# Head sums on four column tiles, constants issued behind x, and the pair's mean taken off by VectorE

## What is computed

```python
x = x + local_attention(_gn(x), ...)       # pool, q k v, 3 x 3 neighbours, softmax, gate, projection
x = x + deformable_conv(_gn(x), ...)       # offsets and masks by a 3 x 3 conv, sampling, ReLU

def _gn(v, G=32, eps=1e-05):               # 64 channels in 32 groups: pairs of channels
    m = jnp.mean(g, axis=(2, 3, 4), keepdims=True)
    s = jnp.var(g, axis=(2, 3, 4), keepdims=True)
    return ((g - m) / jnp.sqrt(s + eps)).reshape(v.shape)

attn = jnp.einsum('bhwnd,bhwknd->bhwnk', qh, kp) * scale    # 8 heads of 8 channels, k: 9 taps
attn = jax.nn.softmax(attn, axis=-1)
out = jnp.einsum('bhwnk,bhwknd->bhwnd', attn, vp)
```

## Time and profile before

| | us |
|---|---|
| median of 3 runs | 197.28 (196.97 to 197.58) |
| profiled execution | 197.45 |
| its span, first to last instruction | 195.4 |
| busy in the span: PE | 174.9 |
| DVE | 152.3 |
| ACT | 103.8 |
| POOL | 86.1 |
| granted TensorE clock, mean over the span | 0.992 |

### The profile page before, as it was taken

How to read it: one execution, slowest core, us unless ns; L and a number is a source line. 1 busy time by engine, 2 the same in 40 slices (tenths; PEclk the granted TensorE clock), 3 DMA queues, 4 the chain that set the end, 5 groups by cost and what they waited for, 6 DMA issues and landing times.

```text
span 195.4 us, 4621 instructions
## 1 busy us (share of the span) xinstructions
PE 174.9 (90%) x1822; PEld 123.9 (63%) x1822; DVE 152.3 (78%) x256; ACT 103.8 (53%) x195; POOL 86.1 (44%) x103
## 2 busy tenths in 40 slices
PE   0299996997979998999999999999989999999990
PEld 0224963653436544547687999658668788998870
DVE  0899958996559798984989988517998897979920
ACT  1136228610002796559877888447938868786000
POOL 8334983569020339504534618403733617536000
PEclk9999999999999999999999999999999999999996
DMA  5950000000040011305551000000012100000000
GB/s 182 351 42 4 3 0 0 3 0 0 0 107 3 27 28 41 98 26 125 122 124 41 15 3 0 3 0 3 9 30 55 37 7 11 0 17 2 20 0 24
DMA packets 10325, 7.66 MB, mean 39 GB/s; under 512 B 5175, under 2 KB 8773, under 8 KB 10297
## 3 DMA queue, kind: packets, MB, share of 16 engines
q1 hardware_dynamic: 9913, 6.35, 12.8%
q10 hardware_dynamic: 288, 0.89, 1.4%
q0 software_dynamic: 96, 0.06, 0.1%
HBM read 2.82 MB, written 0.52 MB: 17 GB/s over the span
## 4 chain that ended last, share of the span: by engine, by line
PE 66%; DVE 14%; ACT 8%; issue 4%; DMA 3%; POOL 2%; SPq 0%; DVEq 0%; POOLq 0%
PE ps L1267 20%; PE ps L1241 11%; PE ps L1161 10%; PE ps L1310 6%; PE ps L1057 4%; DVE smp_prod L801 3%; DMA x_parts<-in_x 3%; PE ps L1226 3%; PE ps L1094 3%; PE ps L1212 2%; ACT disty L616 2%; PE ps L1178 2%; ACT haty L621 1%; PE ps L1025 1%; ACT hx_selx L629 1%
## 5 line engine op out<-in xcount | busy, mean ns | idle before, releaser
L912 DVE TENSOR_TENSOR smp_prod<-ps,hx_selx 128x768 f32<-128x768 f32 x72 | 67.4, 951 | 10.0 <-PE ps L1241 9.2
L1267 PE MATMUL ps<-smp_prod,windows_attention 128*64 128x192 f32 (+2 forms) x512 | 54.9, 337 | 0.1
L1267 PEld LDWEIGHTS ps<-smp_prod,windows_attention 128*64 128x64 f32 x512 | 38.3, 136 | 5.8 <-DVE windows_attention L897 0.4
L1241 PE MATMUL ps<-haty,by_rows 128*64 128x256 f16 x432 | 39.1, 274 | 1.3 <-DVE smp_prod L912 1.2
L476 POOL TENSOR_SCALAR disty<-disty 64x512 f32<-64x512 f32 (+1 forms) x23 | 12.8, 556 | 57.5 <-ACT haty L621 57.4
L1241 PEld LDWEIGHTS ps<-haty,by_rows 128*64 128x64 f16 x432 | 26.6, 109 | 6.4 <-issue 2.7
L629 ACT ACTIVATE hx_selx<-ps 128x512 f32<-128x512 f32 x36 | 21.3, 591 | 16.2 <-PE ps L1226 16.2
L483 POOL TENSOR_TENSOR haty<-disty,haty 64x512 f16<-64x512 f32 (+1 forms) x23 | 24.0, 1043 | 1.9
L1161 PE MATMUL ps<-conv_staged 128*108 128x512 f32 (+1 forms) x60 | 23.3, 521 | 0.7 <-ACT x_parts L593 0.6
L631 ACT ACTIVATE hx_selx<-hx_selx 128x512 f32<-128x512 f32 x36 | 22.7, 631 | 1.1
L926 DVE TENSOR_TENSOR vals_attw<-ps,windows_attention 128x384 f32<-128x384 f32 x24 | 13.3, 555 | 7.1 <-PE ps L1267 4.4
(11 more groups left out here) (139 smaller groups left out, 253.1 us busy)
## 6 DMA issues: line engine op xcount, KB each, us to landing
windows_attention<-windows_attention SPq DMA_DIRECT2D x8, 256.0 KB, 3.8
x_parts<-in_x SPq DMA_DIRECT2D x2, 256.0 KB, 5.2
bcast<-in_bcast SPq DMA_DIRECT2D x2, 256.0 KB, 6.7
x2seq<-x_parts SPq DMA_DIRECT2D x4, 128.0 KB, 2.6
out<-x_parts SPq DMA_DIRECT2D x16, 32.0 KB, 2.0
vals_attw<-in_cf ACTq DMA_DIRECT2D x1, 480.0 KB, 5.8
stack_m<-x_parts SPq DMA_DIRECT2D x12, 36.0 KB
kept<-in_cf ACTq DMA_DIRECT2D x1, 390.5 KB, 4.3
```

The costliest lines, as they stand in the source:

```text
L912: nc.vector.tensor_tensor(pairs, rows, cols.unsqueeze(1).to_broadcast([P, QUARTERS, HW]), ALU.mult).then_inc(s_mult, 1)
L1241: ins = nc.tensor.matmul(ps[h * C:(h + 1) * C, at:at + HW], by_matrix(a, QUARTERS - 1 - k)[:, h * C:(h + 1) * C], haty[i % 2][:, p * HW:(p ...
L1267: return nc.tensor.matmul(dst[:, at:at + strips * 3 * SP].rearrange("p (s k n) -> p s k n", k=3, n=SP), rows, sampled(i, ki, m, first, str ...
```

## The change

1. SP issues `kept` and `attw` right behind x; ScalarE's queue no longer does.
2. In `logits` the four matmuls of a group go to four column tiles (image of the pair and half of the pixels give the tile). The two pairs c now add into the same rows, so that the first matmul in a bank sets `start` and those of c = 1 add to it. `spread` picks its matrices and halves accordingly.
3. The matmul with `gnd` goes. VectorE subtracts its own mean from the pair's mean in PSUM, and copies the pair's mean and variance without waiting for that copy until its last step.

```diff
@@ sync
             for c in range(2):
                 sp.dma_start(xin[:, c * BANK:(c + 1) * BANK], x[:, c * BANK:(c + 1) * BANK]).then_inc(s_x[c], 16)
+            sp.dma_start(kept[:, :], cf[:, 0:kept.shape[1]]).then_inc(s_kept, 16)
+            sp.dma_start(attw, cf[:, kept.shape[1]:]).then_inc(s_cst, 16)
             sp.dma_start(bcast[:, 2 * DG * P:], sel16["bcast"][:, 3 * DG * P:]).then_inc(s_bcast, 16)
@@ scalar
-            act.dma_start(kept[:, :], cf[:, 0:kept.shape[1]]).then_inc(s_kept, 16)
-            act.dma_start(attw, cf[:, kept.shape[1]:]).then_inc(s_cst, 16)
@@ vector, norm
                 dve.wait_ge(s_pair, n)
-                link(nc.vector.tensor_copy(pair[:, :], bank(7)[:, 0:4 * J]))
-                gap = pair[:, 2 * J:4 * J].rearrange("p (j s) -> p j s", s=2)[:, :, 0]
+                own_mean = meanvar[:, :].rearrange("p (j s) -> p j s", s=2)[:, :, 0]
+                mean = bank(7)[:, 0:2 * J].rearrange("p (j s) -> p j s", s=2)[:, :, 0]
+                gap = pair[:, 2 * J:3 * J]
                 var = pair[:, 0:2 * J].rearrange("p (j s) -> p j s", s=2)[:, :, 1]
+                link(nc.vector.tensor_tensor(gap, mean, own_mean, ALU.subtract))
+                nc.vector.tensor_copy(pair[:, 0:2 * J], bank(7)[:, 0:2 * J]).then_inc(s_paircopied, 1)
                 link(nc.vector.tensor_tensor(gap2[:, :], gap, gap, ALU.mult))
+                dve.wait_ge(s_paircopied, n)
@@ tensor, pair_stats
-                nc.tensor.matmul(bank(7)[:, 0:2 * J], gnp, meanvar[:, :], start=True, stop=True)
-                nc.tensor.matmul(bank(7)[:, 2 * J:4 * J], gnd, meanvar[:, :], start=True, stop=True).then_inc(s_pair, 1)
+                nc.tensor.matmul(bank(7)[:, 0:2 * J], gnp, meanvar[:, :], start=True, stop=True).then_inc(s_pair, 1)
@@ tensor, logits
+            FIRST_OF_BANK = (0, TAPS - POOL_TAPS, TAPS - 1)
...
-                for part in range(2):
-                    for j in (2 * c, 2 * c + 1):
-                        ins = nc.tensor.matmul(ps[32 * j:32 * j + 32, t * HF:(t + 1) * HF],
-                                               cst["headsum"][:, 32 * part:32 * part + 32],
-                                               prod[:, t * N + j * HW + part * HF:][:, 0:HF], start=(part == 0),
-                                               stop=(part == 1), skip_group_check=True)
+                for j in (2 * c, 2 * c + 1):
+                    for part in range(2):
+                        rows = 32 * (2 * (j % 2) + part)
+                        ins = nc.tensor.matmul(ps[rows:rows + 32, t * HF:(t + 1) * HF],
+                                               cst["headsum"][:, 32 * c:32 * c + 32],
+                                               prod[:, t * N + j * HW + part * HF:][:, 0:HF], start=(c == 0 and t in FIRST_OF_BANK),
+                                               stop=(c == 1), skip_group_check=True)
@@ tensor, spread
                 for i in range(2 * J):
-                    at = (2 * DG + i % J) * P
+                    j, part = divmod(i, 2)
+                    at = (2 * DG + 2 * part + j // 2) * P
                     ins = nc.tensor.matmul(ps[:, PB[pos % 3] * BANK + i * HF:][:, 0:HF], bcast[:, at:at + P],
-                                           halves[i // J][:, t * HF:(t + 1) * HF], start=True, stop=True)
+                                           halves[j % 2][:, t * HF:(t + 1) * HF], start=True, stop=True)
```

More of the change, by code:

```diff
@@ L150, in bass_local_attention_then_deformable_conv @@
         meanvar = sb("meanvar", [P, 2 * J])
-        pair = sb("pair", [P, 4 * J])
+        pair = sb("pair", [P, 3 * J])
         gap2 = sb("gap2", [P, J])
@@ L282, in bass_local_attention_then_deformable_conv @@
         s_bn = sem("s_bn")
-        s_kept, s_bcast, s_byd, s_selxd, s_own = sem("s_kept"), sem("s_bcast"), sem("s_byd"), sem("s_selxd"), sem("s_own")
+        s_kept, s_paircopied, s_bcast, s_byd, s_selxd, s_own = sem("s_kept"), sem("s_paircopied"), sem("s_bcast"), sem("s_byd"), sem("s_selxd"), sem("s_own")
         s_perm, s_wtap, s_wzero, s_wfin = sem("s_perm"), sem("s_wtap"), sem("s_wzero"), sem("s_wfin")
```

## The result

The changed kernel takes 194.98 us (median of four runs, 194.37 to 195.51), the kernel before on the same chip 197.24 (196.97 to 197.58). The ratio is 0.989 with an interval of 0.987 to 0.992: faster by 2.26 us. The profiled execution took 194.37 us, 3.08 less than that of before. So the median gives less than the profiled execution, and the difference between the two is a question of its own, which the runs answered in part.

A forecast was written before the change was run, and what follows sets the result against it. The prediction took a chain of waits up to 62 us (x's landing, statistics, projections, head sums, pair statistics) as the bound; 1.5 + 1.4 + 0.15 = 3.05 us off 197.45 gave 194.4, 194.2 against the median; eight-in-ten range 193.2 to 196.0.

The forecast's parts named there:

- the idle 0.2 us: At the front, VectorE's wait between the end of L725 and the second statistics of x, expected to vanish.
- the landing of `kept`: Constants behind x: `kept` lands at 5.6 us instead of 5.0, covered with 1.1 us before L1015 needs it.
- the same total traffic: Loads at the front: x first in one queue, with total traffic unchanged, lands its first half at 3.75 us.
- count of 924 kB: Loads at the front: `kept` lands once 924 kB have passed, at 4.9 us, plus 0.65 us until its signal.
- The point from which `kept` costs: At the first group matmul: `kept` would cost time only if it landed later than 6.6 us.
- slower projections: First projections: run 1.65 us longer at TensorE's half speed; 0.15 us charged, 0 to 0.7 kept.
- Rival (a): Loads at the front: the order of issue doesn't matter for x; 195.7 us, chance 0.11.
- Rival (b): Head sums: four column tiles overlap no better than two in a steady stream; 195.6 us, chance 0.09.
- handed on by POOL: Behind the maximum: POOL's first copy of the exponentials starts 0.6 us late, costing about 0.1 us; nothing charged.
- rival (c): TensorE stays at its lower level through projections and head sums; slower, 198.2 us, chance 0.04.
- the clock column in the earlier trace: Ground against the slower case: TensorE's granted clock is 1.00 in a stretch with four matmul records in 2.1 us.
- The forecast's own worst case: Whole kernel: gains at their worst, 1.3 - 0.4 + 1.2 + 0.05 = 2.15 us, giving 195.1 us.

The follow-up runs named there:

- second profile: The changed kernel run again with no edit, on another chip beside the kernel before: 194.22 us, ratio 0.984.
- all together: The changed kernel with `kept` in two loads, three early matmuls on a tile filled by POOL, and `tall` cleared later: 193.58 us, ratio 0.982.

## Why the prediction was right, point by point

**Part 1**, forecast minus 1.5. The mechanism is the one predicted. x landed at 3.45 us instead of the forecast's 3.75, the second half early enough for the idle 0.2 us to go, and the first root moved by 1.77 us in one profile and 1.95 in the other. The step that failed is the landing of `kept`. "At 5.6, covered with 1.1 us" was a single number from a rate; the runs in which it is loaded whole and third in the queue have 5.65, 5.93, 6.20, 6.86, 6.91, 6.99, 7.25 and 7.43. The rate itself was "the same total traffic" as in the earlier trace rows, 373 and 364 kB in the two microseconds that counted. The changed kernel's windows of 1 us from 3.00 (columns as in the earlier trace rows) show less:

```profile
3.00:4.00 1.00, 0.00 (x0) 0.00 (x0) 0.53 (x2) 0.00 (x0) 1.00 (x2) 1.00 0.97 297
4.00:5.00 1.00, 0.00 (x0) 0.00 (x0) 0.96 (x5) 0.86 (x1) 1.00 (x3) 1.00 0.95 279
5.00:6.00 1.00, 0.00 (x0) 0.00 (x0) 0.93 (x4) 0.43 (x1) 1.00 (x2) 1.00 0.70 242
```

In its second profile, where `kept` is early, they moved 265, 349 and 357 kB, and with the constants back on ScalarE's queue 361, 332 and 404. In all eight profiles of the whole load the three windows together move less (730 to 971 kB) than in the three profiles with two queues (1128 before, 1097 with the constants back, and 1113 in the kernel before with its longer norm). By the prediction's count of 924 kB and its 0.65 us, the second profile gives 5.63 and the first 5.9 instead of 6.91, so the lower traffic accounts for a part only.

The point from which `kept` costs was forecast as 6.6 and measured as 6.7 to 6.8, but that is partly luck. The forecast let the group matmul start at 6.7; it could start at 6.35, and VectorE, busy with window sums until 7.5, took up the rest. At 6.91 `kept` cost 0.13 us at the root (the statistics 0.05 later make up the other part of the 0.18 between the two profiles), at 9.25 it cost 2.46. A second term was right in size and wrong in its way: 0.15 us were charged for slower projections as a delay of VectorE's products, but that stretch is 7.10 us before and after. Where they were paid in the changed kernel, it was 0.19 us by way of POOL. The run with `kept` split shows both: 0.38 at the products and 0.37 behind the maximum.

Rival (a) fell with the constants back on ScalarE's queue: the same bytes, another order, and x is 1.75 us later. The Trainium skill ("DMA: Bandwidth & Descriptors", Issuing engines are not separate DMA queues) says that DMAs of several issuers interleave on the same engines, and that agrees with the landing of x at 7.1 in the earlier trace rows. Its next sentence, that issuing from several engines saves sequencer time only, tells less than matters here: which queue the constants stand in decided when the statistics of x could start, at 3.48 or 5.23 us.

**Part 2**, forecast minus 1.4, measured minus 1.35. The last group ends 0.77 us behind the last product, forecast 0.72. Rival (b) fell with the window of 27 records and with the 1.35 us themselves. That the gain isn't handed on by POOL was forecast as well (0.6 us late, "about 0.1 us"), but I charged nothing. Whether it is paid depends on how long ahead of the maximum POOL starts its products, and so on how fast the first projections are. In six profiles on four tiles it starts 8.63 to 8.65 us ahead, and the second root comes 30.49 to 30.51 us behind the maximum. In the changed kernel's second profile it is 8.10 and 30.68, with `kept` split 7.99 and 30.86.

**Part 3**, forecast minus 0.15. The second norm gained 0.16 us. The first lost 0.06 where VectorE was the last to be ready (from the subtraction to the root 0.78 instead of 0.72), and gained some 0.4 where `kept` was late. What the prediction had no term for is the 0.35 us in the sampling part. It goes with VectorE's program. All profiles in which VectorE executes the changed program as it is (after, again, and the undoings that touch only queues, TensorE or POOL) have the product at 40.60, and so has the kernel before with its longer norm. Those with a VectorE program of another length have it at 40.25. Over the seven profiles of each kind the stretch from the convolution's first record to the end is 136.20 us on average with the stall and 135.87 without. The two kinds overlap, 136.00 to 136.62 and 135.66 to 136.15, so one pair says little: the kernel before itself, without the stall, has 136.05. An estimate from these averages is that part 3, with `kept` early, costs -0.16 + 0.06 + 0.33 = 0.23 us. No pair of medians shows that, since the run without part 3 had `kept` late (6.99), where part 3 saves 0.37.

**The sum.** 3.05 us were forecast; the profiled execution gave 3.08, made of -1.77 - 1.35 - 0.16 + 0.23 and 0.03 around the span. That it comes out so well is luck. At the front 1.77 us were gained where 1.5 were forecast: x landed 0.3 us earlier and the 0.15 for the projections weren't paid, less 0.13 for the late `kept` and 0.06 for VectorE's longer norm. The stall gave back 0.23, and the two nearly cancel. The median of the first four runs missed the forecast of 194.2 by 0.8 us and gained 2.26 instead of 3.05. Nothing of rival (c) happened in this profile: no record of the projections is longer than 0.70 us, where before the change some took 1.10, the records of the head sums are 0.27 us long before and after, and L1027, with 1.58 us for two records, is faster than before the change. The prediction's ground against (c), the clock column in the earlier trace rows, was a weak one, as that column prints 1.00 at the lower level too. The forecast's own worst case takes off 0.4 for late projections, where part 1 had kept up to 0.7.

**What stays open.** The first four runs of the changed kernel lie between 194.37 and 195.51, the five of the second job between 194.07 and 194.43. A late `kept` can give such a difference: it moves the root tenth by tenth, and it was at 6.91 in the fastest of the four. But the other three have no profile, so that this is their cause isn't shown. Nor is it shown what makes the same load land anywhere between 5.65 and 7.43 us, or what makes TensorE's level rise during L1027 in one profile and only in the first projections in another. And the medians of the runs with three early matmuls, with the extra memset and with `tall` later are all within 0.3 us of the changed kernel, though their profiled executions are 0.1 to 0.6 below it. With the early matmuls and with the memset the profiled execution is the fastest of its five. Only all together stand clear of it.

## What to carry to other kernels

When loads share the traffic, put first in one queue what the first instruction needs, and read not one landing but several of what now comes behind it: the gain of x was steady, and the price, `kept`, varied by 1.8 us with no edit to it. Try small matmuls on all the column tiles; what is left here on the path is the last group behind the last operand. And before an experiment on a tenth of a microsecond is believed, see where the untouched part stands: here a single instruction more on VectorE moved one wait in it by 0.35 us.

## What was not expected of the hardware

The head sums' records overlapped over four tiles at full pace, one each 25 ns or so, where two tiles gave one each 53 ns.

With all loads in one queue the DMA engines moved 730 to 971 kB from 3 to 6 us, with x and the constants in two queues 1097 to 1128. And yet the statistics of x could start 1.75 us earlier with the one queue.

A stretch of the program that is the same in all kernels contains a wait of VectorE that is either 0.74 or 1.09 us. Adding one memset some 95 us earlier, in idle time, removed it, and adding a copy and a wait to the kernel before brought it in. The work that the product waits for is over 0.11 us ahead of it in the one case and 0.46 in the other. What does this the traces don't show; in these fourteen profiles it goes with VectorE's program ahead of that place and not with what the edit computes.

The run with six early matmuls shows both levels of TensorE's clock (1.2 and 2.4 GHz) in one row of work: the weight loads of its twelve records of 512 columns start 0.85 us apart up to 5.04 us and 0.43 apart from 5.71 on, while the clock column of the windows prints 1.00 throughout, as in the earlier trace rows. The durations of like records show the level there, the column doesn't.
